# Cross-attention over 16 batches on one core: weighing five turns behind the scores, a fourth unit of transposed parts, context loads in six pieces, another prologue

## The reference

```python
q = (x @ Wq + bq).reshape(b, 100, 16, 64)
k = (ctx @ Wk + bk).reshape(b, 1444, 16, 64)
v = (ctx @ Wv + bv).reshape(b, 1444, 16, 64)
attn = softmax(einsum('bqhd,bkhd->bhqk', q, k) / 8)
out = einsum('bhqk,bkhd->bqhd', attn, v).reshape(b, 100, 1024) @ Wo + bo
y = layernorm(x + out) * gamma + beta
```

## Time and profile before

| | us |
|---|---|
| median of 3 runs | 870.71 (869.03 to 873.26) |
| the profiled execution | 871.59 |
| its span | 869.8 |
| PE busy | 846.3 (97%) |
| ACT busy | 779.6 (90%) |
| DVE busy | 774.7 (89%) |
| POOL busy | 569.1 (65%) |

### The profile page before, as it was taken

The page is one execution under the profiler, slowest core; times in us unless marked ns, Lnnn a source line. Parts: engine busy times, 40 slices in busy tenths (PEclk is TensorE's granted clock), DMA queues, the critical chain, the costliest instruction groups (busy, mean ns, idle before and its releaser), DMA issues.

```text
span 869.8 us, 19632 instructions
## 1 busy us (share of the span) xinstructions
PE 846.3 (97%) x7306; PEld 605.2 (70%) x7306; DVE 774.7 (89%) x938; ACT 779.6 (90%) x1132; POOL 569.1 (65%) x575
## 2 busy tenths in 40 slices
PE   7999999999999999999999999999999999999996
PEld 6676776767677766777667776776767777677675
DVE  4988888999989989999899998999899999999984
ACT  5899999989999989999989999998989989999983
POOL 2283997949566693867749586694956669397301
PEclk9999999999999999999999999999999999999999
DMA  7899999999999999999999999999999999999985
GB/s 198 186 211 192 195 210 189 216 200 223 215 209 217 217 204 224 209 226 211 205 213 221 216 208 229 198 227 217 213 215 220 205 233 208 222 188 217 209 183 117
DMA packets 683939, 180.80 MB, mean 208 GB/s; under 512 B 654596, under 2 KB 683076, under 8 KB 683844
## 3 DMA queue, kind: packets, MB, share of 16 engines
q1 hardware_dynamic: 682372, 179.01, 105.7%
q10 hardware_dynamic: 1344, 0.53, 0.3%
q0 software_dynamic: 128, 0.01, 0.0%
HBM read 15.35 MB, written 0.82 MB: 19 GB/s over the span
## 4 chain that ended last, share of the span: by engine, by line
PE 52%; ACT 14%; DVE 13%; DMA 8%; issue 7%; SPq 4%; ACTq 0%; POOLq 0%; POOL 0%; DVEq 0%
PE ps L670 25%; PE ps L631 22%; DMA pt_hi<-p_hi 7%; DVE p_lo L932 6%; ACT p L1072 6%; ACT p_hi L1080 5%; DVE nmax L917 4%; SPq L429 2%; PE ps L495 2%; PE ps L488 2%; SPq L420 1%; ACT unused L1023 1%; DMA bq_pairs<-in_L_xattn_bq_dram 1%; DVE rsum L923 1%; ACT o_t L1110 1%
## 5 line engine op out<-in xcount | busy, mean ns | idle before, releaser
L932 DVE SCALAR_TENSOR_TENSOR p_lo<-p,rinv,p_hi 128x1444 f16<-128x1444 f32 x200 | 370.9, 1855 | 7.5 <-ACT p_hi L1080 7.0
L917 DVE TENSOR_REDUCE nmax<-ps 128x1 f32<-128x1446 f32 x200 | 330.0, 1650 | 18.8 <-PE ps L631 18.3
L1080 ACT ACTIVATE p_hi<-p,rinv 128x1444 f16<-128x1444 f32 x200 | 300.0, 1500 | 32.1 <-DVE rinv L925 28.5
L1072 ACT ACTIVATE p<-ps,nmax 128x1446 f32<-128x1446 f32 x200 | 292.2, 1461 | 17.8 <-DVE nmax L917 15.4
L670 PE MATMUL ps<-pt_hi,c_hi 128*128 128x256 f16 (+1 forms) x1232 | 252.9, 261 | 11.4 <-DMA pt_hi<-p_hi 9.0
L670 PE MATMUL ps<-pt_hi,c_lo 128*128 128x256 f16 (+1 forms) x1232 | 253.0, 261 | 0.0
L631 PE MATMUL ps<-ct_hi,g_hi 128*128 128x482 f16 (+3 forms) x624 | 155.5, 367 | 0.8 <-DVE g_lo L892 0.7
L631 PE MATMUL ps<-ct_lo,g_hi 128*128 128x482 f16 (+3 forms) x624 | 154.9, 366 | 0.0
L631 PE MATMUL ps<-ct_hi,g_lo 128*128 128x482 f16 (+3 forms) x624 | 154.9, 366 | 0.0
L670 PEld LDWEIGHTS ps<-pt_hi,c_hi 128*128 128x128 f16 x1232 | 114.1, 98 | 50.4 <-issue 16.8
L1204 POOL TENSOR_TENSOR g_raw<-g_raw,gb_b 128x400 f32<-128x400 f32 x60 | 81.0, 1350 | 96.2 <-ACT g_raw L1096 96.2
(11 more groups left out here) (138 smaller groups left out, 863.0 us busy)
## 6 DMA issues: line engine op xcount, KB each, us to landing
c_raw<-in_ctx_dram SPq DMA_DIRECT2D x32, 256.0 KB, 6.1
pt_hi<-p_hi SPq DMA_TRANSPOSE x200, 3.5
pt_lo<-p_lo SPq DMA_TRANSPOSE x200, 3.7
c_raw<-in_ctx_dram SPq DMA_DIRECT2D x16, 192.0 KB
c_raw<-in_ctx_dram SPq DMA_DIRECT2D x48, 18.0 KB
out_dram<-late_sb SPq DMA_DIRECT2D x16, 50.0 KB
x_sb<-in_x_dram SPq DMA_DIRECT2D x1, 600.0 KB
o_t<-in_L_xattn_Wq_dram SPq DMA_DIRECT2D x2, 256.0 KB, 4.5
```

What stands on the lines that cost most here:

```text
L917: dve.tensor_reduce(nmax[:, n % RING:n % RING + 1], ps[:, bank:bank + 3, 0:KEYW], AX.XY, ALU.max, negate=True).then_inc(s_nm, 1)
L932: dve.scalar_tensor_tensor(out=p_lo[:, n % LOS, 0:KL], in0=p32[:, n % P32S, 0:KL], scalar=rinv[:, i:i + 1], in1=p_hi[:, par, 0:KL], op0=AL ...
L1072: act.activation(p32[:, n % P32S, :].rearrange("p (k w) -> p k w", w=KEYW), ps[:, bank:bank + 3, 0:KEYW], ACT.Exp, bias=nmax[:, i:i + 1], ...
L1080: act.activation(p_hi[:, par, 0:KL], p32[:, n % P32S, 0:KL], ACT.Copy, scale=rinv[:, i:i + 1]).then_inc(s_hi, 1)
```

## The change

- Weighing lies five turns behind the scores (LAG 4 to 5), and the transposed parts have four units (PTS 3 to 4). PE's loop has one more turn without scores.
- The context of a batch is loaded in six DMAs of two key tiles at r = 0 to 5, in place of three of four tiles at r = 1 to 3. Each half has a semaphore of its own, and each half of the sum waits for its half.
- The three context splits of ACT are at r = 5, 6, 7 (4, 6, 7 before), the two context sums at r = 8, 9 (5, 8), the total at r = 10 (9), the store at r = 10 (2). The first sum of x is at turn 4 (9).
- In the prologue the second two banks of head products are made before the query bias and the transposes of x. ACT empties all four banks of head products, DVE the one with x and the query bias.
- gamma, beta and bo are loaded straight onto 128 partitions by broadcasting DMAs; J_R is left with eight matmuls, and DVE adds bo.

```diff
-    LAG = 4
+    LAG = 5
-    PTS = 3
+    PTS = 4
-    LOADS = 6
+    TL = 2
+    NL = KT // TL
-    LOAD_AT = 1
-    STORE_AT = 2
-    CHI_AT = (4, 6, 7)
+    LOAD_AT = 0
+    STORE_AT = 10
+    CHI_AT = (5, 6, 7)
-    SUM_AT = (5, 8)
-    TOTAL_AT = 9
+    SUM_AT = (8, 9)
+    TOTAL_AT = 10
...
-        J_A, J_X, J_B = 4, 6, 7
-        J_G = J_B + 2
+        J_A, J_B, J_X = 4, 6, 8
+        J_G = J_X + 1
-        BY_SCALAR = [1, 3, J_A, J_A + 1, J_X, J_B + 1, J_V1, J_M2]
+        BY_SCALAR = [1, 3, J_A, J_A + 1, J_B, J_B + 1, J_V1, J_M2]
-        X_SUM_AT = (9, 10)
+        X_SUM_AT = (4, 10)
...
+            def load_context(b, i):
+                load_tiles(b, TL * i, TL * (i + 1), s_c[b % 2][i * SUMS // NL])
...
-                if LOAD_AT <= r < LOAD_AT + NT and w + 2 < B:
+                if LOAD_AT <= r < LOAD_AT + NL and w + 2 < B:
...
             head_products_by_two(w_t[0], w_t[1], 0, J_A)
+            head_products_by_two(w_t[0], w_t[1], 2, J_B)
             query_bias(take(J_X))
             spread_context_max(job_bank(J_G + 2), 0)
             transpose_x(0, J_X).then_inc(s_fill, 1)
-            head_products_by_two(w_t[0], w_t[1], 2, J_B)
...
-                    pe.matmul(bank[:, 0:P], bv_wide[:, c, :], wo_sb[:, c, :], start=(c == 0), stop=False)
-                pe.matmul(bank[:, 0:P], ones_row[:, :], rows_sb[:, 0, :], start=False, stop=True)
-                pe.matmul(bank[:, P:2 * P], ones_row[:, :], rows_sb[:, 1, :], start=True, stop=True)
-                pe.matmul(bank[:, 2 * P:3 * P], ones_row[:, :], rows_sb[:, 2, :], start=True,
-                          stop=True).then_inc(s_fill, 1)
+                    mm = pe.matmul(bank[:, 0:P], bv_wide[:, c, :], wo_sb[:, c, :], start=(c == 0), stop=(c == PAIRS - 1))
+                mm.then_inc(s_fill, 1)
...
-            for n in range(N + 2):
+            for n in range(N + LAG - 2):
...
             def context_sum(b, i):
+                act.wait_ge(s_c[b % 2][i], context_landed(b, i))
                 if i == 0:
-                    act.wait_ge(s_c[b % 2], context_landed(b))
                     act.wait_ge(s_cm, b)
...
-            for i, r in enumerate((bo, gamma, beta)):
-                pool.dma_start(rows_sb[:, i, :], r.rearrange("(o d) -> o d", o=1)).then_inc(s_small, 16)
+            for place, r in ((bo_b[:, :], bo), (rows_b[:, 1, :], gamma), (rows_b[:, 2, :], beta)):
+                pool.dma_start(place, r.rearrange("(o d) -> o d", o=1).to_broadcast([P, D])).then_inc(s_small, 16)
```

More of the change, by code:

```diff
@@ L174, in cross_attention_kernel @@
         g_un = sb("g_un", [P, 1])
-        rows_sb = sb("rows_sb", [1, 3, P])
-        ones_row = sb("ones_row", [1, P])
+        bo_b = sb("bo_b", [P, P])
         table = sb("table", [P, 1])
@@ L227, in cross_attention_kernel @@
         s_cf = [sem(f"first_context_loaded{g}") for g in range(NT)]
-        s_c = [sem(f"context_loaded{i}") for i in range(2)]
+        s_c = [[sem(f"context_loaded{i}_{half}") for half in range(SUMS)] for i in range(2)]
         s_bq = sem("bq_loaded")
@@ L233, in cross_attention_kernel @@
         s_part_id = sem("identity_over_range_ready")
-        s_const = sem("constants_set")
         s_id0 = sem("identity_zeroed")
@@ L353, in every_other, with context_landed @@
             return slice(first, first + 2 * HG - 1, 2)
-        def context_landed(b):
-            return 16 * LOADS * (b // 2 + b % 2)
+        def context_landed(b, half):
+            return 16 * (NL // SUMS + (3 if half == SUMS - 1 else 0)) * (b // 2 + b % 2)
         def emptied(eng, k):
@@ L371, in _, with load_tiles @@
         def _(sp):
[L372 to L377, removed]
+            def load_tiles(b, a, e, landed):
+                par, whole = b % 2, min(e, KT - 1)
+                sp.dma_start(c_raw[:, par, a:whole, :],
+                             ctx_in[b:b + 1, a * P:whole * P, :].rearrange("o (t p) d -> p (o t) d", p=P)).then_inc(landed, 16)
+                if e == KT:
                     tail = ctx_in[b:b + 1, (KT - 1) * P:KL, :].rearrange("o p d -> p o d")
@@ L386, in _ @@
             for g in range(NT):
-                load_context(0, g)
+                load_tiles(0, TG * g, TG * (g + 1), s_cf[g])
             sp.dma_start(x_sb[:, 0:XG, :], x[0:XG, :, :].rearrange("b q d -> q b d")).then_inc(s_x[0], 16)
@@ L391, in _ @@
                 sp.dma_start(w_raw[2][:, cols], Wv[:, cols]).then_inc(s_w[2][half], 16)
-            for g in range(NT):
-                load_context(1, g)
+            for i in range(NL):
+                load_context(1, i)
             def transpose_context_hi(b):
@@ L795, in empty_prologue @@
             elif k == J_R:
-                last = copy(rows_b[:, :, :], split(bank, 3, P))
+                eng.wait_ge(s_small, 16 * 3)
+                last = eng.tensor_tensor(rows_b[:, 0, :], bank[:, 0:P], bo_b[:, :], ALU.add)
             elif k in J_M:
@@ L834, in _ @@
             dve.memset(ax_parts[:, :, :], 0.0).then_inc(s_axz, 1)
-            dve.memset(ones_row[:, :], 1.0).then_inc(s_const, 1)
             def context_max(g):
-                dve.wait_ge(s_cf[g], 16 if g < NT - 1 else 16 * (LOADS - NT + 1))
+                dve.wait_ge(s_cf[g], 16 if g < NT - 1 else 16 * 4)
                 dve.tensor_reduce(c_max[:, g:g + 1], c_raw[:, 0, TG * g:TG * g + TG, :].rearrange("p t d -> p (t d)"),
@@ L876, in _ @@
             context_scale(0, job_bank(J_G + 2))
-            empty(J_B)
+            empty(J_X)
+            dve.tensor_scalar(gb_sb[:, :], job_bank(J_X)[:, XG * QL:XG * QL + H], SCALE, None, ALU.mult).then_inc(s_gb, 1)
             for g in range(NT):
@@ L1038, in a_sum @@
                            ax_parts[:, 0, i:i + 1])
-            for k in (1, 3, J_A, J_A + 1):
+            for k in (1, 3, J_A, J_A + 1, J_B, J_B + 1):
                 empty(k)
             a_sum(0)
-            empty(J_X)
-            act.activation(gb_sb[:, :], job_bank(J_X)[:, XG * QL:XG * QL + H], ACT.Copy, scale=SCALE).then_inc(s_gb, 1)
             for g in range(NT):
                 context_hi(0, g)
-            empty(J_B + 1)
             for g in range(NG):
```

2 lines of the change are left out of this document (removed).

## The result

The changed kernel takes **875.7 us** (median of 20 runs, 872.47 to 878.65) against 870.9 us (20 runs, 868.19 to 875.11) for the kernel before: a ratio of 1.0047 (95% interval 1.0034 to 1.0061). It is slower, by half a per cent, where 1% faster was forecast; the time lies above the forecast range.

What follows compares the result with a forecast made beforehand. PE was taken as the bound between 78 and 847 us, with 12 stalls as real loss. -10.3 + 3.0 + 0.5 - 0.8 = -7.6 us took the median from 870.71 to 863.1 us; own range 860 to 866.5, with rivals 857.5 to 871.

Steps and rivals of the forecast that it cites:

- The prologue, taken as 0: Before the first scores: a 0.6 to 0.75 us gain and 0.9 us of broadcasts taken as equal; -0.8 to +0.6.
- The hoped-for gain of 0.6 to 0.75 us: Prologue: moved head products and earlier context high parts end the first turn 0.6 to 0.75 us sooner.
- The start, taken as 0: From 40 to 78 us: no gain from turn 4 without weighing, since ACT sets the pace; -0.7 to +0.7.
- The 12 stalls, -10.3 us: 78 to 847 us: PE's 12 waits for the high transposed part all go with lag five; bounds 0 and -11.
- Loads in six pieces, 0: SP's queue, each window: three more loads cost 1.7 us of SP's 50 us, nobody waits on them; 0.
- The third rival: Mid-run: transposes fall behind, high parts wait for p_hi's two buffers; +22 or +41 us, to 885 or 904; chance 0.07.
- the 3.6 us that the prediction named as its sign: Mid-run: the prediction is wrong if ACT waits for pt_hi more than 3.6 us.
- The first rival: Mid-run: the softmax chain of ACT and DVE takes over, the 10.3 us return as waits; 872.9, half 867.8; chance 0.14.
- The tail, +3.0: Behind the last scores: one more half unit to weigh, and ACT's copy behind the last high part; +3.0 us.
- J_R, -0.8: In the stretch PE bounds, at 98.95 to 99.82 us: six passes over the three rows go; -0.8 us.
- The moved sums, +0.5: Turns 10 to 1: a context sum moved to r = 9 makes ACT's chain later; +0.5 us, from 0 to +7.

Runs made afterwards that it cites:

- e2: The kernel before, with only the early broadcasts of bo, gamma and beta and the short J_R: 870.56 us, ratio to before 1.0021.
- e10: The kernel before (lag of four) with a third buffer for p_hi: 870.15 us, ratio to before 0.9991.
- e5: e1 with ACT's context splits, sums, total and the sum of x at their old turns, still six loads: 870.98 us, ratio to before 1.0023.
- e8: e4 with a third buffer and semaphore for p_hi: 865.70 us, ratio to before 0.9950.
- e9: e1 with a third buffer for p_hi: 867.91 us, ratio to before 0.9979.
- e11: The kernel after, with the three broadcasts issued at about 22 us, behind the split of the first queries: 870.25 us, ratio to before 0.9996.
- e12: The kernel after with late broadcasts, three loads at r = 1 to 3, third p_hi buffer and e7's tail order: 861.91 us, ratio to before 0.9883.
- e3: e2, but each broadcast replaced by a read of 128 different rows of Wq, same bytes and queue: 868.58 us, ratio to before 0.9984.
- e1: The kernel after, with bo, gamma and beta loaded as one row each and spread by TensorE in J_R, as before: 870.22 us, ratio to before 1.0015.
- e6: e1 with three context loads of four tiles at r = 1 to 3, ACT's new places kept: 865.54 us, ratio to before 0.9951.
- e4: The kernel before with only LAG 5, PTS 4 and one more turn of PE's loop: 869.03 us, ratio to before 0.9987.
- e7: e4 with the copy of the unit of tiles 194 and 195 ahead of ACT's last high part: 866.73 us, ratio to before 0.9963.

## Why the prediction was wrong

**The prologue, taken as 0: this step failed first and by most.** The prediction priced the broadcasts by their bytes, 0.2 MB / 220 GB/s = 0.9 us, set against a gain of 0.6 us, and took the context's last piece for what sets the scale. That piece came 2.95 us later (14.01 against 11.06), but the query bias, which the prediction did not name, was what PE waited for, in the kernel before as well; the scale, whose reciprocal stood at 12.96, was ready 4.5 us later. Here it is in after (DVE's timeline):

```profile
17.44 0.16 DVE L860 RECIPROCAL alpha<-unscale 128x1 f32<-128x1 f32 x1
```

In the two kernels with early broadcasts of one row (after, e2) this reciprocal stands at 17.4 and 16.7; in the other twelve it lies between 12.4 and 13.4. That is 3.3 to 5 us at the scale, of which 1.5 to 1.6 us are the query bias at half clock. The first scores, at 24.1 and 23.7, are 4.2 and 3.8 us later, and that figure has the clock in it as well: after has 10.2 us at half clock from 12.4, and e10, without broadcasts and with its scale at 13.4, has the same and begins its scores at 22.4. Between kernels with equally long half clock, early broadcasts cost 1.8 us at the first scores (after against e10) or 3.1 to 4.0 (e2 against e5, e8, e9, e11 and e12). The Trainium skill, "DMA: Bandwidth & Descriptors", Specifications, names 512 bytes as the smallest transfer that reaches full rate. By that rule these broadcasts, in pieces of 512 bytes, are harmless. e3 agrees with it, and e2, with the same sizes, does not: the rule says nothing of one row that is read 128 times. Why one row is slow, no run here shows.

The hoped-for gain of 0.6 to 0.75 us is there at most in part: e1 and e6, which have the moved head products and the old rows, begin at 19.3 and 19.1, but e5 and e9, with the same prologue, at 20.6 and 19.7, and the kernel before at 19.9. Part of this is the clock (6.8 us at half in e5 and e9, 3.4 in the others), the rest scatter.

**The start, taken as 0: right but for the clock, which made it 1.8 us.** With no weighing in turn 4, PE stands still for DVE's scale. PE's timeline of after:

```profile
42.27 1.32 PE L482 MATMUL ps<-xT,a_sb 128*128 128x100 f32 x8 [2.81 <-DVE unscale L858]
...
43.38 1.41 PE L628 MATMUL ps<-ct_hi,g_hi 128*128 128x482 f16 x3
```

Three score matmuls take 1.41 us here and 0.78 us elsewhere: the granted clock has fallen to half, and stays there for 3.4 us. All kernels with lag 5 have this wait of 2.8 us; after, e1, e6 and e9 show the half clock behind it, e4, e5, e7, e8, e11 and e12 don't. What decides between them was not settled. From the first scores to those of turn 6 it is 23.6 us before, 25.5 in the four with the half clock, and 23.8 in e5, e8, e11 and e12: the standstill by itself costs 0.2 us, the clock behind it the rest. (It is a wait for DVE's scale, not for ACT's banks as forecast.)

**The 12 stalls, -10.3 us: the mechanism right, the sum wrong.** All 12 are gone. The lag alone gained 7.1 us (e4), because "a turn more to land" was counted at PE only. The prediction also followed a late part from its issue only. In 11 of the 12 stalls the high part had stood ready for 0.9 to 4.2 us before SP issued its transpose (2.5 us in the one of the earlier trace rows), and 10 of the 12 concern r = 4, 9 or 10, in the turns after the loads (r = 1 to 3) or the context's transposes (r = 7 and 8) have gone through SP's queue. Another order of that queue was not tried. ACT writes a high part into one of two buffers, and the lag does nothing for these; its waits went from 3.6 to 9.0 us. They come out where ACT is latest, at r = 1 of even windows: the turn there takes 4.66 us on average in e4 and 4.41 in e8, and PE waits for o_t. (Before it took 4.13, but the odd lag puts the longer half of a unit there, and undisturbed such a turn takes 4.34.) With the third buffer (e8) the gain is 10.5 us. That it meets the forecast is in part luck: by the same figures the lag is worth 8.6 us on top of the buffer (e8 against e10).

One such place in after (all engines' timeline), from the late transpose over the wait of ACT to the wait of PE:

```profile
332.32 1.50 SPq L413 DMA_TRANSPOSE ct_lo<-c_lo  x1
...
335.41 1.45 SPq L422 DMA_TRANSPOSE pt_hi<-p_hi  x1
...
340.38 1.50 ACT L1075 ACTIVATE p_hi<-p,rinv 128x1444 f16<-128x1444 f32 x1 [1.38 <-DMA pt_hi<-p_hi]
...
343.37 0.79 PE L628 MATMUL ps<-ct_hi,g_hi 128*128 128x482 f16 x3 [0.55 <-ACT p L1067]
```

A late transpose travels here: the high part that was ready at 332.17 was issued at 335.41, behind a context transpose and a low one, and landed at 340.29; ACT's high part of two turns later waits 1.38 us for that landing, the exponentials stand behind it in ACT's order, and 3 us later PE stands still, 0.55 us, for the banks that they free.

**Loads in six pieces, 0: this step failed.** "Nobody waits on them" is true of the loads' data and false of SP's queue, in which they stand ahead of transposes and leave SP late up to r = 9 (see e6). Six loads together with the moved sums took 3.0 us of what the lag gave (e1 743.5 against e4 740.5), and with the same places three loads are better by 4.9 us. The third rival had this mechanism, by the right buffers; it expected its price at PE at once and far too high (22 to 41 us). ACT's waits for pt_hi, over the 3.6 us that the prediction named as its sign, went to 11.8 us, of which only a part reached PE. The first rival was right about the outlet, ACT, but not about the cause: with the transposes out of the way ACT and DVE do keep up (PE waits 0.3 us in the mid-run of e8, 1.0 in that of e12). The rule of the Trainium skill that was weighed there ("Perfetto Trace Analysis", Identifying the Most-Contended Engine) judges TensorE by two measures, the matmul work against the peak and the weight-load busy time, and the prediction took the second alone, by which ACT stands first. The first one names PE: by an estimate from the trace of the kernel before, its matmuls stream 1.94 million columns, which at a column per cycle of 2.4 GHz (256 columns start 0.109 us apart) are 808 us, 93% of the span. The runs agree with that one; what ACT lacked was buffers.

**The tail, +3.0: right in place, near in size.** Without a fall of the clock it is +2.4 us (19.9 in e1, e4, e6 and e8 against 17.5): the last high part came 6.1 us behind the last scores' start where 6.5 was worked out. In after it is +4.1 us: PE's standstill of 2.3 us is followed by 3.4 us at half clock. PE, ACT and the windows of after (the number behind the five busy times is the granted clock):

```profile
853.02 1.50 ACT L1075 ACTIVATE p_hi<-p,rinv 128x1444 f16<-128x1444 f32 x1 [0.19 <-DVE rinv L923]
854.43 0.45 ACT L1105 ACTIVATE o_t<-ps,unscale 128x256 f32<-128x256 f32 x1
854.94 0.28 PE L667 MATMUL ps<-pt_hi,c_hi 128*128 128x256 f16 x1 [2.29 <-ACT o_t L1105]
...
856.00:860.00 4.00, 4.00 (x25) 3.05 (x24) 0.28 (x1) 0.00 (x0) 0.00 (x0) 0.64 0.83 190
```

The forecast order of events was right (the copy behind the last high part), and a few lines of code take 1.7 us of it back (e7).

**J_R, -0.8: right.** From the scores of turn 17 to those of turn 18 it is 6.55 us before and 5.69 after.

**The moved sums, +0.5: not confirmed.** In the mid-run they cost 2.5 us with six loads, which the medians don't show, and gain 1.9 us with three, which is within the scatter.

In all: the forecast's -7.6 us came out at +3.6 on the spans. Of the difference of 11.2 us, 4.2 lie at the first scores, 1.8 from there to the start of turn 6, 1.1 in the tail, and the rest between turn 6 and the last scores: -6.5 us there, where -10.3 - 0.8 + 0.5 = -10.6 was forecast, so 4.1.

## What to carry to other kernels

A buffer of transposes has two sides: before you give the reader more lag, count the buffers of the writer, and change both or expect the wait to move. When a transfer lands late, look first at how long its data stood ready before the queue issued it. Price a new transfer by whose packets stand beside it and what they read, not by its bytes, and keep broadcasts of one row away from a load that something waits for. Where a step makes an engine stand still, look at the granted clock behind the standstill as well.

## What the hardware showed that was not expected

- Loads that read one row of 512 bytes 128 times slow the others: from 8 to 12 us they held 57.7% of the DMA engines' time for 0.14 MB, where 128 distinct rows took 20.9% for 0.18 MB. From 8 to 9 us all engines moved 126 GB/s at a DMA share of 1.09 in the one case, 233 GB/s at 1.12 in the other.
- Standstills of PE of 2.3 to 2.8 us were followed by 3.4 us at half clock in some kernels and not in others with the same standstill (2.8 us in turn 4: four of ten; 2.3 us in the tail: after, e5, e9 and e11, not e1, e4, e6 and e8).
